# Attention inside a macaron block: banks in a ring of three, row blocks in the order 3, 0, 2, 1, and whole projections

## The reference

```python
x = x + 0.5 * ffn(layernorm(x), w_gate, w_up, w_down)      # silu(gate) * up, 2 of each 4 kept, down
x = x + attn(layernorm(x), w_q, w_kv, w_proj, b_proj)
x = x + 0.5 * ffn(layernorm(x), w_gate, w_up, w_down)

def attn(x):                       # 16 heads of 32 for the queries, one head for keys and values
    q = x @ w_q.T; k, v = split(x @ w_kv.T)
    q, k = rotary(q * s), rotary(k * s)
    p = softmax(where(causal, -max, q @ k.T))      # 512 x 512 for each batch and head
    return (p @ v) @ w_proj.T + b_proj
```

## Time and profile before

| what | value |
|---|---|
| median of 3 runs | 2983.24 us (2978.56 to 2984.75) |
| the profiled execution | 2983.71 us, span of its instructions 2981.9 us |
| first feed-forward phase | about 0 to 1090 us |
| attention, first turned block to last weighed block | 1141.94 to 1876.93 us |
| second feed-forward phase | from about 1899 us |
| busy PE, DVE, ACT, POOL over the span | 94%, 62%, 40%, 5% |
| busy PE, DVE, ACT in 1466.4 to 1560.9 us (one batch of the attention) | 80.0, 54.7, 63.3 of 94.5 us |

### The profile page before, as it was taken

The page is one execution under the profiler, slowest core; times in us unless marked ns, Lnnn a source line. Parts: engine busy times, 40 slices in busy tenths (PEclk is TensorE's granted clock), DMA queues, the critical chain, the costliest instruction groups (busy, mean ns, idle before and its releaser), DMA issues. The chain is left out here.

```text
span 2981.9 us, 41915 instructions
## 1 busy us (share of the span) xinstructions
PE 2794.2 (94%) x15648; PEld 2213.2 (74%) x15648; DVE 1855.5 (62%) x3535; ACT 1200.8 (40%) x2527; POOL 157.0 (5%) x152
## 2 busy tenths in 40 slices
PE   7999999999999977788888887799999999999998
PEld 6888888888888855556555655588888888888887
DVE  5666666666756646555555555476766576676665
ACT  3323233333332315666666677233333333333232
POOL 0000000000000003111111110000000000000000
PEclk9999999999999988999999999899999999999999
DMA  3211211221121020000000000321131112112100
GB/s 131 82 43 57 85 43 46 79 96 49 53 75 43 14 108 1 1 29 11 20 30 29 15 8 16 120 75 49 46 127 43 42 58 85 50 46 90 56 14 29
DMA packets 65021, 156.11 MB, mean 52 GB/s; under 512 B 6864, under 2 KB 6992, under 8 KB 64592
## 3 DMA queue, kind: packets, MB, share of 16 engines
q1 hardware_dynamic: 64848, 153.77, 15.2%
HBM read 128.58 MB, written 25.17 MB: 52 GB/s over the span
## 5 line engine op out<-in xcount | busy, mean ns | idle before, releaser
L346 PE MATMUL bank<-xnt_h,wgu_h 128*128 128x512 f32 x2048 | 803.3, 392 | 10.3 <-issue 7.4
L346 PE MATMUL bank<-xnt_h,wgu_l 128*128 128x512 f32 x2048 | 798.9, 390 | 0.0
L346 PE MATMUL bank<-xnt_l,wgu_h 128*128 128x512 f32 x2048 | 798.4, 390 | 0.0
L503 DVE TENSOR_TENSOR h<-bank,sg 128x512 f32<-128x512 f32 x256 | 176.9, 691 | 600.4 <-PE bank L346 585.9
L346 PEld LDWEIGHTS bank<-xnt_h,wgu_h 128*128 128x128 f32 x2048 | 385.6, 188 | 91.5 <-issue 9.0
L442 ACT ACTIVATE mag<-h 128x512 f32<-128x512 f32 x256 | 162.0, 633 | 702.6 <-DVE h L503 702.6
L346 PEld LDWEIGHTS bank<-xnt_h,wgu_l 128*128 128x128 f32 x2048 | 385.3, 188 | 80.3
L346 PEld LDWEIGHTS bank<-xnt_l,wgu_h 128*128 128x128 f32 x2048 | 385.7, 188 | 79.2
L365 PE MATMUL bank<-wd_h,hs_h 128*128 128x512 f32 x1024 | 400.5, 391 | 9.1 <-DVE hs_l L538 9.1
L365 PE MATMUL bank<-wd_l,hs_h 128*128 128x512 f32 x1024 | 400.1, 391 | 0.0
L365 PE MATMUL bank<-wd_h,hs_l 128*128 128x512 f32 x1024 | 400.0, 391 | 0.0
(11 more groups left out here) (105 smaller groups left out, 3090.7 us busy)
## 6 DMA issues: line engine op xcount, KB each, us to landing
raw_gu<-in_w_gu SPq DMA_DIRECT2D x128, 512.0 KB, 5.0
raw_d<-in_w_d SPq DMA_DIRECT2D x128, 256.0 KB, 2.6
x_mid<-x_sb SPq DMA_DIRECT2D x64, 256.0 KB, 2.0
x_sb<-in_x SPq DMA_DIRECT2D x32, 256.0 KB, 4.9
x_sb<-x_mid SPq DMA_DIRECT2D x8, 1024.0 KB, 5.8
x_sb<-x_mid SPq DMA_DIRECT2D x32, 256.0 KB, 5.1
out<-x_sb SPq DMA_DIRECT2D x32, 256.0 KB, 2.1
probs<-in_w_q SPq DMA_DIRECT2D x1, 1024.0 KB, 4.8
```

The source lines that it names most:

```text
L346: last = pe.matmul(ps, w[:, r, kind, k], xs[:, b, k], start=(i == 0), stop=(i == 3 * KD - 1))
L503: v.tensor_tensor(h[:, r], bank[UP + r % 2][:, :], sg[:, r % 2], ALU.mult).then_inc(h_done, 1)
```

## The change

It touches the attention phase alone.

- The ring of banks has three banks (4, 5, 7); the bank `spare` is gone, and every projection takes a turn of the ring and is done in one piece, twelve matmuls, at most one in a step (`PROJECT`): keys and values at k = 0, queries at 1, 3, 5, 7, output at 9, 11, 13, 15.
- The row blocks of a group come in the order 3, 0, 2, 1. A step on PE is: up to three blocks turned, `weigh(K - 1)`, the fourth block, the projection, the sums or layer-norm tile, `scores(K + 3)`.
- Scores are three steps ahead instead of two; `probs` and `nmax` have three copies. DVE masks heads 0, 1, copies block 1, then masks heads 2, 3. ACT takes the exponentials of heads 2, 3 of K + 1 and heads 0, 1 of K + 2. DVE also copies block 3.
- DVE copies a query projection to `qraw` (one instruction) and POOL does the whole rotation (four); for batch 0 DVE rotates as before. POOL also widens the sums and makes the high part of the output (both were ACT's). `qt` has one copy instead of two.
- `turn_sums` moves to the end of the group's last step. Layer-norm tiles are turned one in a step, at k = 11 to 14, for the batch after next, and those of batch 1 ahead of the first step.

```diff
-            ON_VECTOR = ((), (1,), (1,), (1,))
-            TURN_X, TURN_KV, TURN_K, TURN_Q = (0, 1), 3, 6, (10, 11)
-            ROTATE = {5: 0, 6: 1, 8: 2, 9: 3}
-            SUM = {11: 0, 12: 1, 14: 2, 15: 3}
-            STATS = {7: (0,), 10: (1,), 13: (2, 3)}
+            turning = (bank[4], bank[5], bank[7])
+            AHEAD = 3
+            ORDER = (3, 0, 2, 1)
+            ON_VECTOR = ((), (1,), (1,), (1, 3))
+            TURN_X, TURN_KV, TURN_K, TURN_Q = {11: 0, 12: 1, 13: 2, 14: 3}, 1, 4, {10: (0, 1), 12: (2, 3)}
+            PROJECT = {0: ("kv", 0), 1: ("q", 0), 3: ("q", 1), 5: ("q", 2), 7: ("q", 3),
+                       9: ("out", 0), 11: ("out", 1), 13: ("out", 2), 15: ("out", 3)}
+            STATS = {3: 0, 5: 1, 7: 2, 8: 3}
+            ROTATE = {2: 0, 4: 1, 6: 2, 8: 3}
...
 gpsimd
+                    def rotate_q(B, t):
+                        n = B * TT + t
+                        g.wait_ge(q_copied, n - TT + 1)
+                        g.wait_ge(q_finished, n)
...
+                        g.tensor_tensor(heads_of(qrot[:, t]), q, cos, ALU.mult).then_inc(q_rotated, 1)
+                        g.tensor_tensor(tmp[:, :, 0:HALF], q[:, :, HALF:HD], sin[:, :, 0:HALF], ALU.mult).then_inc(q_rotated, 1)
+                        g.tensor_tensor(tmp[:, :, HALF:HD], q[:, :, 0:HALF], sin[:, :, HALF:HD], ALU.mult).then_inc(q_rotated, 1)
+                        finish_q(B, t)
...
                         if k % TT == 1 and K > TT:
-                            low_output(K // TT - 1)
+                            part_output(K // TT - 1)
+                        if k % TT == 2:
+                            widen(K // TT)
...
 tensor
                     def step(K):
                         B, k = divmod(K, UNITS)
-                        i, nxt = k % TT, B + 1
-                        side(K, 0)
-                        if i == 0 and K > 0:
-                            turn_sums(K // TT - 1)
-                        turn_probs(K, 0)
-                        if i >= 1:
-                            turn_probs(K, 1)
-                        side(K, 1)
+                        i, nxt = row_of(K), B + 1
+                        for j in range(0, min(i, 2) + 1):
+                            turn_probs(K, j)
                         if K > 0:
                             weigh(K - 1)
-                        for j in range(2, i + 1):
-                            turn_probs(K, j)
-                        side(K, 2)
-                        if K + 2 < ALL:
-                            scores(K + 2)
-                        side(K, 3)
+                        if i == 3:
+                            turn_probs(K, 3)
+                        project(B, k)
+                        if k % TT == TT - 1:
+                            turn_sums(K // TT)
+                        if nxt + 1 < BATCHES and k in TURN_X:
+                            turn_x(nxt + 1, TURN_X[k])
...
+                        if K + AHEAD < ALL:
+                            scores(K + AHEAD)
+                        if nxt < BATCHES:
+                            for hg in TURN_Q.get(k, ()):
+                                turn_q(nxt, hg)
...
 scalar
-                        exps(K + 1, 0)
...
+                        exps(K + 1, 2)
+                        copy_turned(K, 0)
+                        exps(K + 1, 3)
+                        if 2 in mine:
+                            copy_turned(K, 2)
+                        exps(K + 2, 0)
+                        exps(K + 2, 1)
...
 vector
                     def step(K):
...
+                        mask_scores(K + AHEAD - 1, (0, 1))
+                        if 1 in ON_VECTOR[i]:
+                            copy_turned(K, 1)
+                        mask_scores(K + AHEAD - 1, (2, 3))
+                        if nxt + 1 < BATCHES and k - 1 in TURN_X:
+                            lo_x(nxt + 1, TURN_X[k - 1])
+                        if nxt < BATCHES and k == TURN_KV + 1:
+                            keys(nxt)
+                        if 3 in ON_VECTOR[i]:
+                            copy_turned(K, 3)
+                        drain_projection(B, k)
+                        if k % TT == TT - 2:
                             invert_sums(K // TT)
...
+                        if k % TT == 0 and K > 0:
                             scale_output(K // TT - 1)
...
```

More of the change, by code:

```diff
@@ L646, in attention_phase @@
             ALL = BATCHES * UNITS
-            SCORES, TURNS = 0, 4
-            outs, spare = bank[6], bank[7]
+            SCORES = 0
+            outs = bank[6]
+            turning = (bank[4], bank[5], bank[7])
             HALF = HD // 2
@@ L671, in blocks_before @@
             def blocks_before(K, of):
-                one = [sum(1 for j in range(i + 1) if of(i, j)) for i in range(TT)]
+                one = [sum(1 for j in range(i + 1) if of(i, j)) for i in ORDER]
                 return K // TT * sum(one) + sum(one[:K % TT])
@@ L685, in copies_of, with next_turn @@
             def copies_of(K, j):
[L687 removed]
+                i = row_of(K)
+                mine = by_vector if by_vector(i, j) else by_scalar
                 return (pt_vector if mine is by_vector else pt_scalar,
[L689 removed]
+                        blocks_before(K, mine) + sum(1 for n in range(j + 1) if mine(i, n)))
             bank_of = {}
[L693 to L694 removed]
+            def next_turn(*key):
+                bank_of[key] = turning[len(bank_of) % len(turning)]
@@ L882, in scores @@
                             rows = slice(s * HD, (s + 1) * HD)
-                            last = pe.matmul(bank[SCORES + s][:, 0:width(i)], qt[rows, B % 2, hg, i * P:(i + 1) * P],
+                            last = pe.matmul(bank[SCORES + s][:, 0:width(i)], qt[rows, hg, i * P:(i + 1) * P],
                                              kt[rows, B % 2, 0:width(i)], start=True, stop=True)
@@ new lines, in project_out, with project @@
+                        for k in range(KD):
+                            for n, (a, w) in enumerate(((h_of, wp_h), (h_of, wp_l), (l_of, wp_h))):
+                                last = pe.matmul(ps[:, :], a[:, k, tok], w[:, k], start=(k == n == 0),
+                                                 stop=(k == KD - 1 and n == 2))
+                        last.then_inc(proj_done, 1)
+                    def project(B, k):
+                        if k not in PROJECT:
+                            return
+                        what, t = PROJECT[k]
+                        if what == "out":
+                            if B > 0:
+                                project_out(B - 1, t, take_turn(("out", B - 1, t), x_summed, (B - 1) * TT + t + 1))
+                        elif B + 1 < BATCHES:
+                            if what == "kv":
+                                project_kv(B + 1)
+                            else:
+                                project_q(B + 1, t)
@@ L997, in _ @@
                     for t in range(TT):
-                        for k in range(KD):
-                            project_out(BATCHES - 1, t, k, bank[SCORES + t])
+                        project_out(BATCHES - 1, t, bank[SCORES + t])
                 @blk.scalar
@@ L1173, in add_output, with drain_projection @@
                         v.tensor_tensor(x_of(B, t), x_of(B, t), ps[:, :], ALU.add).then_inc(x_summed, 1)
+                    def drain_projection(B, k):
+                        if k not in PROJECT:
+                            return
+                        what, t = PROJECT[k]
+                        if what == "q" and B + 1 < BATCHES:
+                            copy_q(B + 1, t)
+                        if what == "out" and B > 0:
+                            add_output(B - 1, t, bank_of["out", B - 1, t])
```

349 lines of the change are left out of this document (160 added, 189 removed).

## The result

| | median | runs | ratio to the kernel before, 95% interval |
|---|---|---|---|
| before | 2981.09 us | 2978.56 to 2984.75, 4 runs | |
| after | 2945.51 us | 2943.57 to 2947.03, 4 runs | 0.9879 [0.9862, 0.9896] |

The change is faster by 1.2%. The profiled execution took 2943.57 us (span 2941.8), 40.1 us of span less than before. The last weighed block ends at 1837 instead of 1877 us, so the feed-forward phases take no part in it.

What follows compares the result with a forecast made beforehand. PE's order and its waits in the attention (735 of 2982 us) were taken as the bound. Gains of 50 us, less 2 for the clock and 6 ahead of the first step, made 42, taken as 40: 2944 us, range 2914 to 2972.

Steps and rivals of the forecast that it cites:

- The group: Four attention steps with two projections: 19.05 us against 22.6, with a new 1.5 us wait for DVE's masks; 13.6 without projections.
- The tiles: Layer-norm tiles at k = 11 to 14: banks wait for DVE's low part, 9.4 us a batch, bounds 2.6 and 15.
- The list of signs: Expected in the profile: attention about 693 us instead of 735, wait ahead of projections gone, low-part wait 5 to 7 a batch.
- The batch: One attention batch: 89.9 us, 92 with 2 us for the clock, against 95.5; batches 1 to 5 gain 18 us.
- Ahead of the first step: Before the attention loop: query tiles turned from about 1128, first turned block at 1148 instead of 1141.9, 6 us lost.
- Cutting projections less finely gives nearly nothing by itself: Projections on PE: issuing them in larger pieces counted as zero, from prices of rows following each other.
- POOL: Rotation, widening and high part moved to POOL: some 20 us more per batch, near 37 in all, hidden.
- ACT: ACT in a group of four attention steps: needs some 12.6 us, so it doesn't take over.
- Smaller DVE waits: Attention: half of the mask wait and tiles' waits vanish, 40 us over seven batches, 2904 us; chance 0.12.
- POOL slows DVE: Nine DVE normalisations and key instructions a batch lengthened by up to 0.6 us each, 20 us, 2964; chance 0.12.
- The clock: Waits leave TensorE at half clock for whole projections, 5.2 us instead of 2.9; slower, up to 3017; chance 0.08.
- Nothing changes: Layer-norm tiles' banks wait at the upper bound, 5.6 us a batch, 35 in all: 2979 us; chance 0.05.

Runs made afterwards that it cites:

- low-part experiment: The kernel after, with DVE's low part of the fresh layer-norm tile moved right behind the first two masks of its step: 2900.66 us, ratio 0.9732.

## Why the prediction was right

It said 2944 us, 2914 to 2972. Measured were 2945.5. Point by point:

- **The group** (19.05): 19.23 at 1438.28. DVE's masks behind its copy are waited for 1.44 to 1.53 us (1.5 predicted) ahead of the scores of 128 columns. The group without projections, 13.6, measured 13.61, and not by errors that cancel: its turned blocks start at 1775.39, 1778.86, 1781.99, 1785.74 and 1789.00, so the four steps take 3.47, 3.13, 3.75 and 3.26 us, where 3.4, 3.2, 3.75 and 3.3 were predicted. These two came from chains of starts, not from durations, and hold to 1%.
- **The tiles**: waits of 2.4, 2.0, 2.3 and 1.0 us predicted at k = 12 to 15, measured 2.34, 1.80, 2.83 and 0.47. The low-part experiment shows the cause: order on DVE. The terms listed for these steps add up to 10.3 us (7.7 of waits, 1.76, 0.86), where the text says 9.4, without the overlap that would explain it. From 1294.22 to 1323.97 the four steps take 29.75 us, 10.7 more than 19.05, and some 1.5 of that are rows at the half level; so 9.4 was nearer than its listed terms. The list of signs has the wait ahead of projections gone; at k = 15 it is there, 3.3 us from 1170 to 1760 us, as the walk of the steps had it.
- **The batch** (92): 91.2, 92.5, 93.4, 92.0 and 92.0, together 17.7 us gained where the sum had 18. The rest of the stage gained 31 us, where it had 30 (12 for batch 6, 20 for batches 0 and 7, less 2 for the clock).
- **Ahead of the first step**: query tiles turned at 1127.8 (1128 predicted), first block at 1150.3 (1148), so 8.4 us lost and not 6. The stage ended 7 us shorter than I wrote (686 for 693): the sentence on what would show it added the 6 us a second time, which the sum did not. That the total agrees to 1.5 us is luck: this loss was 2.4 us larger than predicted, and the 2 us taken off for small waits made up for it.
- **"Cutting projections less finely gives nearly nothing by itself"** is the statement that failed. It weighed only how rows follow each other on PE. In the kernel before, whole projections cost 61 us, since the quarters cover waits. The total came out right because I had walked the changed group with its own waits, and didn't add this zero to the old group.
- **POOL**: 37 us a batch predicted, 32.4 measured. The widening and the high part take 0.64 and 0.66 us, half of the 1.3 that I took from a product with two inputs. It was hidden either way. The Trainium skill ("GPSIMD Engine Reference", 3.1 Elementwise — side-by-side cycle accounting) gives 2.6 cycles an element for two inputs and 1.03 for the shortest bodies, at 1.2 GHz an estimate of 1.11 and 0.44 us for 512 columns without the dispatch. The rows are some 0.2 us above both, 1.28 and 0.61 to 0.66, and from 256 to 512 columns the two-input rows grow by 0.54 us, where 2.6 cycles make an estimate of 0.55; so the trace agrees, and no row here shows what the 0.2 us are.
- **ACT** was right to be left out: 0.6 us twice a group put back on it changed nothing.

The rivals. *Smaller DVE waits* fell: they were there at full size, and it took another order to remove them. *POOL slows DVE* fell as a cost, though the effect exists (below): with the rotation back on DVE the kernel is slower, not faster. *The clock* was partly right: it takes some 3 us of busy time a batch (I had 2), in rows behind the waits of k = 12 to 14, but no projection of the middle groups ran at the half level. One of k = 13 began at it (1307.09), and only its first matmul. *Nothing changes* fell.

What isn't settled: from the kernel before with whole projections (3041) to the change (2945) there are 96 us. POOL's rotation is worth 11 of them, ACT's relief about nothing; the third bank is worth 35 and the look-ahead about nothing where the low part is early, and neither was measured without that. The new order of rows is worth less than nothing, as measured with the low part early. The rest lies in the tiles one by one, the places of the projection and the sums in the step and the shares of DVE and ACT, which were not tried one at a time. That the clock falls because of the waits is argued, from rows at the half level that stand in the steps of these waits, and from the batch at 1.00 once the tiles' waits are under 1.2 us. Why the same wait is followed by such rows in one batch and not in another stays open.

## What to carry to other kernels

Walk the changed loop as chains between the engines' starts, and price every instruction that stands ahead of the awaited one on the other engine: here the order of three items on DVE was worth 45 us and the order of the row blocks another 38, each more than the whole change (36). Work in the middle of a step is cover; before making it whole, look up which wait stands at each place that it leaves. When an experiment takes one thing back, look at what it puts ahead of what, or a misplaced instruction is read as the price of the thing.

## What I had not expected of the hardware

**A wait can be paid twice, by the clock.** In the change a batch has 7.4 us of waits between k = 12 and 15 (the rows above), the longest 2.83, and a granted clock of 0.95 to 0.98. With the low part early no wait of a batch is over 1.52 us and the clock is 1.00, and PE's busy time for the same instructions falls from 80.05 to 77.14 us. In the kernel without the third bank the waits in these steps still add up to 5.3 us, none over 1.46, and its clock is 1.00 too.

**DVE and POOL.** POOL's row of four bias additions, then DVE's rows in the same microseconds (start, duration), in the kernel after:

```profile
1204.70 5.17 POOL L776 TENSOR_TENSOR x_sb<-x_sb,bias 128x512 f32<-128x512 f32 x4
```

```profile
1203.81 0.45 DVE L233 TENSOR_SCALAR xn<-x_sb,meanvar,rstd 128x512 f32<-128x512 f32 x1
...
1206.85 0.28 DVE L1176 CUSTOM_DVE_ANT_0 probs<-bank,causal 128x128 f32<-128x128 f32 x1
...
1207.27 1.47 DVE L233 TENSOR_SCALAR xn<-x_sb,meanvar,rstd 128x512 f32<-128x512 f32 x1
```

The mask at 1206.85 (0.28) is as long as anywhere. The normalisation at 1207.27, SBUF to SBUF, took 1.47 us; the one at 1203.81, beside no addition, 0.45. It is the only one of 24 in 1150 to 1760 us that took so long, and the only one that met an addition; of the three that met one earlier, at 1129.75 and 1133.78, each took about 1.4. Beside the copy L805 and the cast L811 it is POOL that is longer: 0.77 and 0.85 us instead of 0.61, with the normalisation started 0.15 us ahead of it and taking 0.45 to 0.54. The Trainium skill ("GPSIMD Engine Reference", 1. Specifications) has DVE and POOL share SBUF interfaces, with contention for DVE instructions in a 2-port mode or with two SBUF inputs; the trace agrees for the masks, which have one input in a bank, and for the normalisation if it runs in such a mode, which no row shows. The price was 1.0 us, less than one addition of POOL (1.29).
